# A router's logits with the gate held in the array, a scalar recurrence moved to ScalarE, and loop bodies in a new order

## The reference, cut to what matters

```python
# x, ctx: (32, 512, 512)
s = sigmoid(norm(query));  for _ in range(10): s = 3.9 * s * (1.0 - s)     # one number a token
q = query * (1.0 + 0.1 * (s - 0.5)) * (1.0 + 0.1 * wave)
mem = memory * const
Q, K, V = q @ Wq.T + bq, mem @ Wk.T + bk, mem @ Wv.T + bv
Qf, Kf, Vf = fft(Q), fft(K), fft(V)              # along the 512 positions
attended = ifft(hamilton(hamilton(Qf*f, Kf*f), Vf*f)).real
x = x + attended
t = layer_norm(layernorm(x))
logits = t @ gate_weight.T                       # 8 experts
# top-1, softmax weight, rank in the expert (capacity 1024), scatter into slots
h = gelu(dispatch @ wi);  out = x_normed + weight * (h @ wo)    # 8 experts, 512 -> 2048 -> 512
x = x + out
```

## Time and profile before

| | |
|---|---|
| median of 3 runs | 3581.08 us (3577.95 to 3581.91) |
| the profiled execution's own time | 3578.17 us |
| its span, first to last instruction | 3576.3 us |
| mean granted TensorE clock | 0.984 of full |
| PE / DVE / ACT / POOL busy over the span | 97% / 72% / 42% / 52% |
| stage 1 | about 0 to 2119 us |
| stage 2 | about 2121 to 3576 us |

### The profile page before, as it was taken

One profiled execution on the slowest core, in us unless ns is written; L12 is line 12 of the kernel. 1 busy time (PEld: TensorE's weight loads), 2 busy tenths in 40 slices (PEclk: granted clock), 3 DMA queues, 4 the chain that ended last, 5 costly groups with the idle time before them and its releaser, 6 DMA issues. The chain is left out here.

```text
span 3576.3 us, 48219 instructions
## 1 busy us (share of the span) xinstructions
PE 3452.6 (97%) x15056; PEld 2631.2 (74%) x15056; DVE 2559.9 (72%) x3536; ACT 1513.5 (42%) x2598; POOL 1845.3 (52%) x2985
## 2 busy tenths in 40 slices
PE   6999999999999999999999949999999999999998
PEld 4677776777776777766777638888888888888886
DVE  3999999999999999989999944444444444444443
ACT  4444545455454544545445333333333333333332
POOL 4788888888888888888888630000000000000000
PEclk8999999999999999999999969999999999999999
DMA  5422221222112221222221223333333333333331
GB/s 186 161 84 80 78 69 59 71 83 71 59 59 71 83 71 59 83 71 71 71 71 60 72 71 106 107 115 119 118 120 120 119 118 107 106 107 119 108 109 42
DMA packets 223387, 326.67 MB, mean 91 GB/s; under 512 B 36832, under 2 KB 102624, under 8 KB 223232
## 3 DMA queue, kind: packets, MB, share of 16 engines
q1 hardware_dynamic: 207904, 307.97, 25.4%
q0 software_dynamic: 15360, 16.99, 1.4%
HBM read 256.82 MB, written 101.97 MB: 100 GB/s over the span
## 5 line engine op out<-in xcount | busy, mean ns | idle before, releaser
L1196 POOL TENSOR_TENSOR tally<-tally,unit 1x1 f32<-1x1 f32 x16 | 2.9, 182 | 1356.5 <-DVE mixed L1377 1356.5
L1304 ACT ACTIVATE act<-hid_ps 128x512 f32<-128x512 f32 x256 | 153.1, 598 | 801.4 <-PE hid_ps L1235 801.4
L1365 DVE CAST act_h<-act 128x512 fp32r<-128x512 f32 x256 | 109.3, 427 | 527.0 <-ACT act L1304 527.0
L442 PE MATMUL pair<-w_q,q_spec 128*128 128x512 f32 x1024 | 464.8, 597 | 8.3 <-ACT q_spec L627 8.0
L1235 PE MATMUL hid_ps<-tok_h,w_h 128*128 128x512 f32 x1024 | 405.6, 396 | 2.9 <-DVE tok_l L1353 2.4
L1235 PE MATMUL hid_ps<-tok_l,w_h 128*128 128x512 f32 x1024 | 399.6, 390 | 0.0
L1235 PE MATMUL hid_ps<-tok_h,w_l 128*128 128x512 f32 x1024 | 399.2, 390 | 0.0
L1251 PE MATMUL out_ps<-w_l,act_h 128*128 128x512 f32 x1024 | 398.6, 389 | 0.0
L1249 PE MATMUL out_ps<-w_h,act_h 128*128 128x512 f32 x1024 | 398.3, 389 | 0.0
L1250 PE MATMUL out_ps<-w_h,act_l 128*128 128x512 f32 x1024 | 398.3, 389 | 0.0
L1359 DVE TENSOR_TENSOR w_l<-w_raw,w_h 128x2048 fp32r<-128x2048 f32 x128 | 293.4, 2293 | 90.8 <-ACT w_h L1298 90.8
(11 more groups left out here) (177 smaller groups left out, 8344.4 us busy)
## 6 DMA issues: line engine op xcount, KB each, us to landing
w_raw<-in_L_ffn_wi SPq DMA_DIRECT2D x128, 512.0 KB, 3.4
w_raw<-in_L_ffn_wo SPq DMA_DIRECT2D x128, 512.0 KB, 4.5
w_raw<-in_x SPq DMA_DIRECT2D x32, 1024.0 KB, 5.1
w_raw<-in_ctx SPq DMA_DIRECT2D x32, 1024.0 KB
x_res<-in_x SPq DMA_DIRECT2D x31, 1024.0 KB, 5.2
out<-x_res SPq DMA_DIRECT2D x31, 1024.0 KB, 4.3
slots<-rows SPq DMA_DIRECT2D x4, 4160.0 KB, 17.0
got<-slots SPq DMA_DIRECT2D x16, 1040.0 KB, 7.6
```

Of the source, the lines that this page charges most:

```text
L442: last = nc.tensor.matmul(pair[k % 2][:, s, :], spec[:, c, tile * 256 + s * P:tile * 256 + (s + 1) * P], w[:, c, :], start=(c == 0 and n = ...
L1196: nc.gpsimd.tensor_tensor(tally[:], tally[:], unit[:], ALU.add).then_inc(tallied, 1)
L1304: nc.scalar.activation(act32[i % 2][:], hid_ps[i % 2][:], ACT.Gelu).then_inc(gelu, 1)
L1365: v.tensor_copy(act_h[i % 4][:], act32[i % 2][:]).then_inc(ah_ready, 1)
```

## The change

1. `logits` is done from the other side. The gate is padded from 8 to 32 columns (`gate_w`), and each of its four 128x32 blocks is the stationary operand in one of four column groups of the array. Two token tiles at once (256 columns) are streamed past each: 8 matmuls instead of 16. The four groups write four partial sums into four quarters of `even_ps`' partitions. ScalarE copies that bank (`logits_out`), and `logits_turn`, 4 new matmuls, sums the four quarters and turns them to token rows at once, with a constant 0/1 matrix `chosen` (8 columns), into a corner of `odd_ps`.
2. The recurrence s -> 3.9 s (1 - s) becomes y -> (c - 3.9 y)^2 in shifted form: ten small Square activations on ScalarE (`logistic`), one waiting for the other, and one Exp (`decay`). GpSimd's `stats1` is cut into three pieces (`stats1`, `start1`, `scales1`), 46 steps becoming 15, with ScalarE in between.
3. `real_bins` handles both bins in one instruction: 27 steps become 15.
4. The bodies of all five engines are written in a new order; the lag of some steps grows by one body. On SP, the DMAs of the small path and of the residual of the last sequence go ahead of the store of the last but one.
5. At the start, the weights of K and V are scaled and rounded in one pass (2 activations instead of 4) that stands behind the first spectrum and not ahead of it; the low halves take the scale as well.
6. Stage 2's first group is loaded in four pieces, and `norm`, `turn` and the first `up` wait for them piece by piece.

```diff
-                    def logits(b, t):
-                        pe.wait_ge(g_ev, b * 4 + t + 1)
-                        if t == 0:
+                    def logits(b, h):
+                        pe.wait_ge(g_ev, b * 4 + 2 * h + 2)
+                        if h == 0:
                             pe.wait_ge(unfold, b * UNF + UNF)
                         for c in range(CB):
-                            last = nc.tensor.matmul(even_ps[:, t * EXPERTS:(t + 1) * EXPERTS], x_tok_t[t % 2][:, c, :],
-                                                    gate_g[:, c, :], start=(c == 0), stop=(c == CB - 1))
+                            last = nc.tensor.matmul(even_ps[32 * c:32 * c + 32, h * 256:h * 256 + 256], gate_w[:, c, :],
+                                                    x_tok_t[:, :, c, :], start=True, stop=True, tile_position=(0, 32 * c))
                         last.then_inc(logit_mm, 1)
+                    def logits_turn(b):
+                        pe.wait_ge(logit_ev, b + 1)
+                        for t in range(ROWT):
+                            o = LOGITS + t * EXPERTS
+                            last = nc.tensor.matmul(odd_ps[:, o:o + EXPERTS], parts[:, t * P:(t + 1) * P], chosen[:],
+                                                    start=True, stop=True)
+                        last.then_inc(logit_ready, 1)
...
+                    def logistic(b):
+                        act.wait_ge(stat1, b * STAT1 + 10)
+                        nc.scalar.activation(map_y[0][:], map_s[:], ACT.Square,
+                                             bias=const["minus_half"][:, 0:1]).then_inc(mapped, 1)
+                        for n in range(1, MAP_STEPS):
+                            act.wait_ge(mapped, b * MAPPED + 1 + n)
+                            nc.scalar.activation(map_y[n % 2][:], map_y[(n - 1) % 2][:], ACT.Square,
+                                                 bias=const["centre"][:, 0:1], scale=-R_MAP).then_inc(mapped, 1)
...
+                    def logits_out(b):
+                        act.wait_ge(logit_mm, b * 2 + 2)
+                        nc.scalar.activation(parts, even_ps[:], ACT.Copy).then_inc(logit_ev, 1)
```

More of the change, by code:

```diff
@@ L530, in body @@
[L530 to L534, removed]
+                        project(b - 1, 1, 0)
+                        logits(b - 3, 0)
                         turn(b - 3, 1 - p, 2)
-                        logits(b - 3, 0)
-                        project(b - 1, 0, 1)
                         turn(b - 3, 1 - p, 3)
+                        project(b - 1, 1, 1)
@@ L552, in _ @@
+                        project(b - 1, 4, 1)
+                        inverse(b - 2, 1, 0)
+                        dft(b, 1, 3)
+                        project(b - 1, 5, 0)
+                        inverse(b - 2, 1, 1)
+                        project(b - 1, 5, 1)
+                        turn(b - 2, p, 0)
+                        project(b, 0, 0)
+                        turn(b - 2, p, 1)
+                        project(b, 0, 1)
                     for b in range(6):
@@ L705, in body @@
                         token_block(b - 3, 1)
+                        decay(b)
+                        squares_x2(b - 3, 1 - p)
+                        real_part(b - 1, 0)
+                        logistic(b)
+                        token_block(b - 3, 2)
+                        real_bin(b - 1, 0)
+                        token_block(b - 3, 3)
+                        spectrum(b, 0, 0)
+                        real_part(b - 1, 1)
+                        real_bin(b - 1, 1)
+                        spectrum(b, 0, 1)
+                        q_of(b)
+                        real_part(b - 1, 2)
+                        logits_out(b - 3)
+                        base_of(b - 3, 1 - p)
+                        real_bin(b - 1, 2)
+                        spectrum(b, 0, 2)
                     for b in range(7):
@@ new lines, in body @@
+                        sums(b - 3, 4)
+                        convert(b - 2, 0)
+                        products(b - 3, 5)
+                        convert(b - 2, 1)
+                        sums(b - 3, 5)
+                        folds_q(b - 1)
+                        folds_c(b)
+                        choose(b - 4, p)
+                        back_to_parts(b - 3, 1)
+                        convert(b - 2, 2)
+                        products(b - 2, 1)
+                        place(b - 4, p)
@@ L1092, in _ @@
+                    for b in range(29, BATCH + 4):
                         body(b, b % 2)
@@ L1143, in experts @@
         got_in = [sem(f"got_in{i}") for i in (0, 1)]
+        got_first = [sem(f"got_first{t}") for t in range(GT)]
         wh_ready, wl_ready = sem("wh_ready"), sem("wl_ready")
@@ L1223, in up @@
                     n = group(e, g)
-                    if i == 0:
+                    first = isinstance(n, int) and n == 0 and i == 0
+                    if i == 0 and not first:
                         pe.wait_ge(tl_ready, n * CB + CB)
```

321 lines of the change are left out of this document (174 added, 147 removed).

## The result

The changed kernel takes 3621.96 us (median of 5 runs, 3619.12 to 3644.31), the kernel before 3580.50 on the same chip (5 runs, 3577.95 to 3581.91): ratio 1.0135, 95% interval 1.0103 to 1.0166. It is slower by 1.35%, where I had forecast 3524 and given "slower" 0.07. The profiled execution took 3639.95 us, 0.5% above its median, that of before 3578.17.

What follows compares the result with a forecast made beforehand. Stage 1 was taken as bound by TensorE's stream. 39 us over 31 sequences plus 8, 6 and 4 at the ends made 57 off 3578.2: 3521, with the median's 2.9 above it 3524 us (3505 to 3549).

Steps and rivals of the forecast that it cites:

- the small path: SP's new DMA order: r_spec lands some 5 us ahead of inverse(b,0,0), so no wait of PE was counted.
- Rival C: GpSimd and ScalarE delay token_block, PE waits 3.1 us ahead of its dft: 65.8 us a sequence, 3630 us; chance 0.07.
- the 18 us of the ends: Gains outside the steady part: fill 8, end of stage 1 6, start of stage 2 4 us.
- The bound before: Stage 1 of the kernel before is bound by PE's stream, 62.55 of 63.63 us a sequence; VectorE is next.
- TensorE's wait and clock: Before dft(b,0,0): 0.83 us idle and 0.25 us of lower clock a sequence, both counted as gone.
- The logits: On PE, 3.32 us a sequence replaced by 2.1 for column groups, 0.85 for logits_turn, 0.2 for switches; stream 62.38.
- A: Rival: the column groups don't overlap; logits matmuls 3.36 us, period stays at 63.63, 3563 us; chance 0.18.
- B: Rival: all four column groups overlap; logits matmuls 0.84 us, stream 61.12 us a sequence, 3485 us; chance 0.20.
- The wait for token block 2: PE's wait at dft(b,0,0) for ScalarE's token_block goes; ten Squares take 2.6 us, about 1 us of room left.
- The fill: Start of stage 1: q's scale ready at 24, first K projection at about 54; 8 us less (4 to 10).
- The end of stage 1: The small path's last DMA goes ahead of a store, slot computation next within 1 us: 6 us less (3 to 8).
- The start of stage 2: norm starts 2 us earlier, first up with the first of four pieces: together 4 us less (1 to 5).

Runs made afterwards that it cites:

- e1: The changed kernel with real_store(b-4) moved to the head of SyncE's body, nothing else touched: 3499.12 us, ratio 0.9776.
- e2: The changed kernel with only real_store(b-4) and load_c(b) exchanged in SyncE's body, so r_spec's store goes first: 3502.02 us, ratio 0.9784.
- e3: The changed kernel with real_out and real_spread ahead of store and load_x on SyncE, real_store still behind load_c: 3605.14 us, ratio 1.0068.
- e6: e1 with the logits as before (16 matmuls of 8 columns, no eviction, no logits_turn): 3521.15 us, ratio 0.9837.
- e9: The kernel before with the recurrence on GpSimd cut from 10 steps to 2, nothing else: 3532.92 us, ratio 0.9872.
- e11: e1 with token_block(b-3,2) ahead of logistic(b) and token_block(b-3,3) ahead of real_bin(b-1,0) on ScalarE: 3485.18 us, ratio 0.9738.
- e5: e1 with the logistic recurrence back on GpSimd, 10 steps: 3842.89 us, ratio 1.0737.
- e7: e1 with decay and logistic earlier on ScalarE, start1 ahead of mean2 and scales1 ahead of stats2 on GpSimd: 3498.75 us, ratio 0.9775.

## Why the prediction was wrong

**The step that failed** is the small path: "r_spec lands some 5 us ahead of `inverse(b,0,0)`. If that room went, PE would wait by the difference." It landed 3.1 us behind it. I had written the SP list down and saw what heads it; the 5 us have no sum behind them, and I did not count what each entry sends. By the changed kernel's rows the store goes at 1385.15 and the inverse is due at 1396.05, 10.9 us later. r_spec stands behind three 1 MB transfers and a wait for a fourth, small one that itself stands behind two of them: 9.7 us to its issue and 4.4 to its landing. e1, e2 and e3 show it. The lower clock after the idle then makes some 2 us more in ten of 18 periods and 3.4 in three. My list of signs had "VectorE or a DMA is where I was wrong"; it was not in the rivals, and it should have been the rival on the slower side.

Rival C had priced a wait of 3.1 us at another place: 65.8 us a sequence and 3630. Measured are 65.5 (2031.6 / 31) and 3622. That is luck: C's stream was 1.3 us too long, and it took 0.3 for the lower clock. Its "From a wait of 2.1 us on, it is slower than before" does not follow either: by its own terms the 18 us of the ends are used up at a wait of 1.5 us.

**The bound before.** That PE's stream is 62.55 us was nearly right in size; that "stage 1 is bound by it" was wrong. The stream is 62.2 (e6 and e9, both 100% busy; e9's `choose` from 925.3 to 1484.7 in nine periods is 62.16). The other 1.5 us of the 63.63 were GpSimd's, and by the waits it reached TensorE by way of ScalarE: "they are not on the path in the steady part, and freed time there is worth nothing by itself" is refuted by e9, 46 us. 1.1 of these 1.5 us were booked as TensorE's wait and clock and counted as gone; the changed kernel took them away by another way than I said, with the squares on ScalarE.

**The logits.** Four matmuls of one `logits`, e1's PE timeline:

```profile
1335.91 0.64 PE L534 MATMUL even_ps<-x_tok_t,gate_w 128*32 128x256 f32 x8
1336.48 1.09 PE L523 MATMUL xt_ps<-eye,rows 128*128 128x128 f32 x8
...
1340.57 1.99 PE L449 MATMUL xt_ps<-fwd,c_fold 128*128 128x256 f32 x8 [0.26 <-ACT x_tok_t L726]
1342.49 0.64 PE L534 MATMUL even_ps<-x_tok_t,gate_w 128*32 128x256 f32 x8
1343.06 1.99 PE L449 MATMUL xt_ps<-fwd,c_fold 128*128 128x256 f32 x8
...
1350.38 3.61 PE L449 MATMUL xt_ps<-fwd,c_fold 128*128 128x256 f32 x16
1353.83 0.95 PE L544 MATMUL odd_ps<-chosen,x_tok_t 128*128 128x8 f32 x8
1354.64 3.68 PE L475 MATMUL pair<-w_q,q_spec 128*128 128x512 f32 x8
```

Eight records take 1336.48 - 1335.91 = 0.57 us, not 1.05 (A 1.7, B 0.4): 1.14 a sequence for my 2.1. Cut into windows of 0.05 us, the trace has four records at work in the first window and the other four from 0.25 us on. So they run as two rounds of four at once, and my picture, in which only the second record of one group and the first of the next overlap, was wrong. logits_turn is 0.81 (0.85 said). The rest is what the switches cost. The stream fell from 62.2 to 61.07. The old logits are 3.4 in e6, twice 1.70 (3.32 in the old order, where they stand in three places), so 2.3 was added, 0.3 of it neither matmuls nor turn; I had 0.2. Two of the four pauses can be read: 1342.49 - 1340.57 is 1.92, where each of the two dfts ahead of `logits_turn` takes 3.45 / 2 = 1.73 from start to start, and 1335.91 comes 0.09 after the last K record's 0.23. The Trainium skill ("TensorEngine Tiling (Array Packing)", Key Properties) has a drain at each change of mode; pauses of this size agree with it. The same skill ("TensorE: Matmul & The Clock Gate", Part 3) has 2.38x for three column tiles; here four gave 8 x 0.21 / 0.57 = 2.9. So the new stream was mis-sized by 1.3 us, 41 us in all, in the kernel's favour, close to B's 61.12, and it did not show until r_spec was on time. Some 0.35 of the 1.3 was in the stream before.

**The wait for token block 2.** Called gone, it is 0.42 us in e1: the ten squares take 3.24 us, not 2.6 (0.32 each where I had 0.26), and ScalarE waits 0.65 us for GpSimd's map_s ahead of them. e11 shows what it was worth, 14 us. "VectorE stays hidden down to a period of some 61" held: 61.07 in e11, with VectorE 521 of 554 us busy. Rival C did not come; the path that it names, from GpSimd over ScalarE to TensorE, is real, though, as e5 shows with a longer chain.

**The fill**: 8 us said, 9.6 measured, by the steps given (q_bias at 24.12 for 24, the first K projection at 53.74 for 54):

```profile
53.74 0.80 PE L475 MATMUL pair<-w_kh,c_high 128*128 128x512 f32 x1 [6.07 <-DVE w_vl L970]
```

**The end of stage 1**: 6 said, 0 measured. SyncE does send r_spec early, at 2136.60; from the last sequence's first K projection to its inverse it is 2157.22 - 2085.38 = 71.8 us, as before (2087.51 - 2015.74). The step was that the slot computation comes "within 1 us": that `choose` holds the `ranks` ahead of the inverse by 8.6 us. PE's waits, 1900 to 2260 us:

```profile
PE odd_ps L558 <- DVE onehot L1118: 10.2, 2, 8.6
...
PE even_ps L509 <- DVE s L1054: 6.7, 1, 6.7
```

**The start of stage 2**: 4 said; from that inverse to the first `up` 42.98 in place of 48.98, 6.0 less. The three ends together were 18, and the profiled executions have 9.6 + 7.8 = 17.4; with one of the three at nothing, that is luck.

Without the failed step the forecast of 3524 stands 0.7% above e1's 3499, the kernel that it describes: it counts too little gain for the logits, and too much for the last wait and the end of stage 1.

## What to carry to other kernels

When bodies are put in a new order, walk every small DMA that an engine waits for as if it were an instruction: count the megabytes issued ahead of it in the same stretch, at the rate at which the trace moves them, and add what its issuing engine waits for before it gets there. Issue the small ones first. And before a stream is called the bound, ask every engine's waits, also of those at 40%: an engine that is busy 56 of 63 us in one dependent chain can set the pace without ever being named in the waits of the engine that looks bound; a kernel that leaves most of that chain out tells it in one run.

## What the runs showed of the hardware

- 4 KB took at most 1.9 us to land with nothing large issued just ahead (e2), 4.4 us behind 1 MB issued 0.6 us before (the changed kernel), and 8.2 us behind 3 MB issued in the 2.7 us before (e3).
- Four column groups of 32 with 256 float32 columns work side by side: 0.57 us for eight records that cost 0.21 each on the whole array, so 2.9 at a time where four would be full.
- An idle stretch in a stream that is busy otherwise brought the granted clock down to 0.50 in some periods only. In the changed kernel 13 of 18 had it, after 2.8 to 3.7 us idle, for about 3.5 us (ten) or 7 us (three); five were spared, after 2.6 to 3.1 us. In e3, with 2.6 to 3.0 us idle in every period, it fell in two periods, was spared in the next two, and so on through all 18. So the length of the idle stretch alone does not decide it; what does stays open.
- Ten dependent Squares of 128x4 on ScalarE take 0.32 us each. Beside VectorE's two-input operations of 2048 elements, a GpSimd addition that takes 0.20 us alone took 2.21, and a power that takes 1.01 alone took 2.93 (e7; alone at the changed kernel's start, 18.35 and 18.63 us).
